# Multiplying zeros in eight waits of TensorE, in a four-round transformer kernel

## The reference, cut to what matters

```
x = x + layernorm(L0_attn(layernorm(x)))   # state-space mixer (conv, chunked scan, gate), then an FFN of 1024
x = x + layernorm(L0_ffn(layernorm(x)))    # x @ W.T plus a top-2-of-8 low-rank sum of rank 16
x = x + layernorm(L1_attn(layernorm(x)))   # causal attention, 16 heads of 16
x = x + layernorm(L1_ffn(layernorm(x)))    # top-4-of-64 experts of 64, capacity 32, plus two shared experts
```

## Time and profile before

| what | value |
|---|---|
| time, median of 3 runs | 1124.2 us (1123.39 to 1128.37) |
| profiled execution, first to last instruction | 1143.5 us |
| PE busy | 1018.9 us, 89% of the span |
| DVE, ACT, POOL busy | 782.8, 548.9, 394.8 us |
| mean granted TensorE clock | 0.958 |
| PE's share of the chain that ended last | 64% |

### The profile page before, as it was taken

How to read it: one execution, slowest core, us unless ns; L and a number is a source line. 1 busy time by engine, 2 the same in 40 slices (tenths; PEclk the granted TensorE clock), 3 DMA queues, 4 the chain that set the end, 5 groups by cost and what they waited for, 6 DMA issues and landing times.

```text
span 1143.5 us, 21218 instructions
## 1 busy us (share of the span) xinstructions
PE 1018.9 (89%) x7808; PEld 620.7 (54%) x7808; DVE 782.8 (68%) x1759; ACT 548.9 (48%) x1158; POOL 394.8 (35%) x605
## 2 busy tenths in 40 slices
PE   6999897899999998989998998999998998976466
PEld 3454554654555666654555666654555676655342
DVE  4888525678888646678887546779896546766135
ACT  3888411346887211456886212447986112421112
POOL 3566201132765101133674101234673001223442
PEclk9999898899999999999999999999998999988778
DMA  6889200003443000004443001004348304024727
GB/s 212 314 295 312 79 1 19 1 2 106 140 143 116 1 1 19 20 1 141 142 126 95 1 1 38 1 13 155 131 143 200 68 1 129 1 68 116 220 107 299
DMA packets 74743, 113.64 MB, mean 99 GB/s; under 512 B 6167, under 2 KB 64670, under 8 KB 73744
## 3 DMA queue, kind: packets, MB, share of 16 engines
q1 hardware_dynamic: 71952, 104.48, 29.3%
q0 software_dynamic: 1536, 3.60, 1.1%
q10 hardware_dynamic: 1152, 4.19, 0.9%
HBM read 93.46 MB, written 19.40 MB: 99 GB/s over the span
## 4 chain that ended last, share of the span: by engine, by line
PE 64%; DVE 14%; issue 8%; ACT 7%; POOL 3%; DMA 2%; another core or an unknown queue 2%; SPq 0%; DVEq 0%; POOLq 0%; ACTq 0%
PE bank L957 25%; PE bank L1033 4%; PE bank L1124 4%; PE bank L1280 3%; PE bank L1238 3%; PE bank L1141 3%; DVE hf L1830 2%; PE bank L970 2%; PE bank L1324 2%; PE bank L1327 2%; POOL rs L1656 2%; PE bank L1048 2%; PE bank L948 2%; PE bank L1379 1%
## 5 line engine op out<-in xcount | busy, mean ns | idle before, releaser
L957 PE MATMUL bank<-uT,w_in 128*128 128x512 f32 (+1 forms) x584 | 273.9, 608 | 6.2 <-DVE hf L1844 3.0
L1830 DVE SCALAR_TENSOR_TENSOR hf<-bank,conv_w,hf 128x510 f32<-128x510 f32 (+2 forms) x224 | 162.6, 744 | 34.6 <-ACT nmax L1504 20.0
L957 PEld LDWEIGHTS bank<-uT,w_in 128*128 128x128 f32 (+1 forms) x584 | 102.2, 188 | 126.1 <-issue 91.1
L1656 POOL TENSOR_TENSOR rs<-ve,half 128x2 f32<-128x2 f32 x56 | 39.0, 697 | 289.2 <-DVE ve L1974 289.1
L1487 ACT ACTIVATE hf<-bank,conv_b,conv_w 128x512 f32<-128x512 f32 x128 | 99.2, 775 | 53.1 <-PE bank L957 52.6
L1124 PE MATMUL bank<-hf 64*64 64x128 f32 (+3 forms) x2048 | 89.5, 308 | 14.4 <-issue 7.5
L1124 PEld LDWEIGHTS bank<-hf 64*64 64x64 f32 x2048 | 75.6, 135 | 44.4 <-issue 37.6
L957 PE MATMUL bank<-uT,w_gu 128*128 128x512 f32 x224 | 99.0, 593 | 0.0
L1465 ACT ACTIVATE xc<-bank 128x512 f32<-128x512 f32 x44 | 26.3, 597 | 119.3 <-PE bank L957 77.1
L2271 DVE TENSOR_REDUCE nmax<-bank 128x2 f32<-128x256 f32 (+1 forms) x128 | 65.4, 553 | 20.3 <-PE bank L1327 18.1
L957 PEld LDWEIGHTS bank<-uT,w_gu 128*128 128x128 f32 x224 | 42.3, 190 | 46.6 <-issue 45.9
(11 more groups left out here) (343 smaller groups left out, 2170.8 us busy)
## 6 DMA issues: line engine op xcount, KB each, us to landing
hf<-cum_dram SPq DMA_DIRECT2D x32, 384.0 KB, 3.5
dec<-cum_dram SPq DMA_DIRECT2D x32, 384.0 KB, 4.0
tmp<-cum_dram SPq DMA_DIRECT2D x32, 384.0 KB, 3.5
x<-cum_dram SPq DMA_DIRECT2D x32, 384.0 KB, 3.9
y_dram<-xf SPq DMA_DIRECT2D x16, 512.0 KB, 6.1
w_in<-in_w_in SPq DMA_DIRECT2D x1, 3584.0 KB, 11.7
w_in<-in_w_egu SPq DMA_DIRECT2D x6, 512.0 KB, 10.4
w_in<-y_dram ACTq DMA_DIRECT2D x5, 512.0 KB, 10.8
```

The costliest lines, as they stand in the source:

```text
L957: mm = pe.matmul(plan[key][0:n, :], w[:, k, cols], uT[:, k, :], start=k == 0, stop=k == DC - 1)
L1656: pool.tensor_tensor(rs[:, cols], ve[:, cols], half[:, cols], ALU.pow).then_inc(rstd_ready.sem, 1)
L1830: ins = dve.scalar_tensor_tensor(d, x, conv_w[:, j, TAPS - 1 - s:TAPS - s], d, ALU.mult, ALU.add)
```

## The change

A helper `multiply_zeros(key, n, r)` waits for its bank, issues `n` bf16 products of the zero tile with 512 zero columns, and raises the bank's counts itself, so that no other engine takes part. It is called at eight places of TensorE's program, with 79 products in all: 10 in the first round between `project_out` and the FFN's transposes; 12 in the first round's low-rank stage before the second half's transposes, and 5 and 16 after the last product of its first and of its second half; in the last round 8 at step 19 of the attention loop, 9 after the loop and before `add_o(7)`, 7 after the shared experts' first half, and 12 between `shared_down(0)` and `add_to_table`. Bank 6 or 7 holds the results, which nobody reads. Nothing is removed or moved.

```diff
+            if r == 0:
+                plan.use("zeros_ffn", 6, r)
             for j in range(2):
                 plan.use(("O", j), j, r)
...
+            if r == 0:
+                for n in range(3):
+                    plan.use(("zeros_lora", n), 7, r)
             plan.use(("T", "att", 0), 6, r)
...
             plan.use(("W", 0), 7, r)
+            if r == LAST:
+                for n in range(2):
+                    plan.use(("zeros_att", n), 6, r)
...
         plan.use(("W", 1), 6, LAST)
+        plan.use(("zeros_att", 2), 6, LAST)
         plan.use(("T", "moe", 1), 6, LAST)
...
         plan.use("pos", 6, LAST)
+        plan.use(("zeros_att", 3), 6, LAST)
         plan.use("table", 7, LAST)
...
+            def multiply_zeros(key, n, r):
+
+                pe.wait_ge(*plan.before(key, r))
+                for i in range(n):
+                    mm = pe.matmul(plan.of(key, r)[:, :], zeros_bf[:, :], zeros_wide, start=True, stop=True)
+                    if i == n - 2:
+                        mm.then_inc(plan.fills(key, r), 1)
+                mm.then_inc(plan.drains(key, r), 1)
...
                     for j in range(2):
                         route(j, r - 1)
+                else:
+                    multiply_zeros("zeros_ffn", 10, r)
                 for j in range(2):
                     transposes(pe, "ffn", 1, u, j, r)
...
+                    elif j == 1:
+                        multiply_zeros(("zeros_lora", 0), 12, r)
                     transposes(pe, "lora", 2, u, j, r)
...
+                    if r == 0:
+                        multiply_zeros(("zeros_lora", 1 + j), (5, 16)[j], r)
                     if r > 0 and j == 0:
                         shared_down(0, r - 1, (1,))
...
+                    if n == 19 and r == LAST:
+                        multiply_zeros(("zeros_att", 0), 8, r)
...
+                if r == LAST:
+                    multiply_zeros(("zeros_att", 1), 9, r)
                 add_o(7)
                 transposes(pe, "moe", 4, xf, 0, r)
...
             for g in range(2):
                 shared_hidden(g, 0, LAST)
+            multiply_zeros(("zeros_att", 2), 7, LAST)
             transposes(pe, "moe", 4, xf, 1, LAST)
...
             shared_down(0, LAST)
+            multiply_zeros(("zeros_att", 3), 12, LAST)
             add_to_table(LAST)
             shared_down(1, LAST)
```

## The result

The changed kernel takes 1117.8 us (median of 8 runs), the kernel before 1123.8 us beside it; the ratio is 0.9931, with a 95% interval of 0.9911 to 0.995. By the ratio that is 7.7 us faster, with 5.6 to 10.0 us by its interval; the two medians by themselves lie 6.0 us apart. The forecast was 10.5 us and 1113.7 us, with a range of 1110 to 1119.5: the direction and the range held, the size was 2.8 us too large. A second measurement of the same kernel, further down, gave 0.9935.

The account below looks back on a forecast made before the run. The prediction took TensorE as the bound, busy 89% of the span and slowed by clock falls after waits. Terms of 2.0 + 6.0 + 1.3 + 1.2 = 10.5 us took the 1124.2 us median to 1113.7 us, range 1110 to 1119.5.

Parts of the forecast that it names:

- Term 1: First round's scan end: the FFN's first products run at the full clock, 2.0 us gained, at least 0.9.
- The row that spoke against it: Second round's scan end: `route` filled the wait, yet the clock fell for 3.42 us and the products took 4.85 us.
- Terms 2 and 3: First round's low-rank stage: second-half product 2.7 us faster, queries and keys 2.8, transposes at most 0.5; together 6.0 us.
- Term 4: Last round's `project_o(1)`: its 8 products fall from 3.19 to 1.9 us, 1.3 us gained.
- Term 5: Last round's `shared_down(1)`: 6.09 us falls to 3.72; counted as 1.2 us, between 0 and 2.4.
- POOL's limit: Tail: after the last gather at 1067.35 us, POOL's 16 scatters cannot end before 1089.2 us.
- the pairs' line: Tail: ACT's copy of `shared_down(1)`, then its exponentials and first expert pair; if it ends last, 2.4 us count.
- its inference about the unknown waits: Tail of the profiled execution: 19.25 us of wait without known releaser, inferred to be absent from timed runs.
- Some falls stay: Rival: the clock still falls where transposes and short waits follow the zeros; 1117 to 1120 us, chance 0.22.
- The gain is hidden: Rival: later rounds or the tail absorb gains; 1116.2 us without the last round's; hidden within 0.5%, chance 0.08.
- The blocks delay TensorE: Rival: blocks begun at the lower clock outlast their waits by 5.8 us, 1130 us; chance 0.04, shared with zeros doing nothing.
- Zeros are no work for the clock: Rival: nothing is gained, 1124 to 1130 us; chance 0.04, shared with blocks that delay.

Follow-up runs that it names:

- narrow: The change with all 79 products cut to 8 columns in place of 512; ratio 0.9995 to the kernel before.
- last_only: The change with only the 36 products of the last round, none in the first; ratio 0.9981 to the kernel before.
- scan_zeros: The change plus zeros at scan ends: 8 before the last convolution (all rounds), 2 and 3 around the FFN transposes (rounds 2 to 4); 1113.76 us, ratio 0.9904.
- pairs_late: The change plus 16 products of zeros between `shared_down(1)` and the expert pairs; ratio 0.9927 to the kernel before.
- again: The changed kernel itself, unaltered, measured and traced a second time; 1117.67 us, ratio 0.9935 to the kernel before.
- double: The change with twice the products in each of the eight blocks, 158 in all; ratio 1.0041 to the kernel before.
- tail_zeros: The change plus 52 products of zeros in the tail's wait for the loads of `y_dram`; ratio 0.9922 to the kernel before.

## Why the prediction was right, and where it was off

**The mechanism** held: zeros in the waits keep the clock, and without their columns (`narrow`) nothing is left of the gain.

**Term 1, scan end, 2.0 us.** L980 takes 3.62 us, against 5.71. From the start of `project_out`'s last products (L1219 in the changed kernel) to the end of the start column it takes 10.37 us in the nine traces with this block at its length, 12.05 in three of the four without and 12.87 in before's: 1.7 to 2.5 us, 1.9 on average. (The start column differs by as much, 138.2 against 140.1 us on average, but also holds what comes before, such as a fall within the scan in `last_only`.) The row that spoke against it was the second round's, where `route` fills the wait and the clock fell. The Trainium skill, "TensorE: Matmul & The Clock Gate", section "Part 4: PE-mode transpose", says that a transpose does not count as busy in the way that a product does; by it this term was 0.9. The measurement decides against that here: behind ten zeros the clock outlasted eight transposes and a wait of 0.85 us, in all nine traces (L980 3.62 us). At the other scan ends a fall at the transposes did occur (370.60 and 872.36 us above), though not in the third round of the same execution, and with the zeros of `scan_zeros` it is gone; which of those zeros it takes, and whether the transposes or the waits beside them let the clock fall, no run here shows.

**Terms 2 and 3, low rank, 6.0 us.** 72.6 to 66.5 us, 6.2 in each of the traces. Its parts don't stand apart as the prediction had them: the 12 alone are worth 3.8 us, the 5 and the 16 alone 4.6, together 6.2, not 8.4.

**Term 4, `project_o(1)`, 1.3 us.** 1.2: L1404 takes 1.99 us against 3.19.

**Term 5, `shared_down(1)`, 1.2 us.** This is the step that failed, as a size. In the profiled execution L1067 does take 3.69 us in the place of 6.09, 2.4 us, and none of it counts: POOL's line ends last, with room to spare (`pairs_late`, and `again` with 6.70 us and a tail no longer). The prediction had both lines, knew POOL's limit, and took the middle between 0 and 2.4 because the timed median agreed with the pairs' line. The lower end, 0, was right. So was its doubt that the clock may still fall in the 2.46 us wait, and its inference about the unknown waits.

**What the sum left out.** 1.9 + 6.2 + 1.2 are 9.3 us, and 7.7 were measured. The interval of 5.6 to 10.0 us holds both, so it is not shown that anything is missing. Of the other columns, route is 0.1 us longer with the last round's blocks, which is the 0.15 us wait behind the 7. Rounds 2 to 4 had 733.7 to 736.8 us in the three traces without the first round's blocks and without scan zeros, 735.0 to 738.2 in the seven with the first round's blocks; the means differ by 1.3 us, and the traces by 3.3 falls against 4.6 on average. The tail is 0.6 us longer on average in the traces with the 12 full-width products just ahead of it than in those without, before's own left out. Together that is 2.0 us, about the 1.6 between the two, but in both the sets of traces overlap, so it is not shown that the change causes more falls or a longer tail. The falls at the scan ends of rounds 2 to 4 come in different numbers in each execution, and the prediction said that they make runs differ by several us; it didn't put them into the sum.

**The rivals.** *Some falls stay* didn't come true at the places of the change: the stretches named by it are at 1.00. *The gain is hidden* came true for one term. It priced the last round's whole gain as lost, 1116.2 us, and the outcome, 1124.2 less 7.7 or 1116.5 us on the same base, lies by it, though project_o's 1.2 us do arrive. *The blocks delay TensorE* would have needed the lower clock ahead of a block; in the changed kernel no block began at it. What late blocks cost, `double` shows. *Zeros are no work for the clock* fell with the first window. Two small sums of these parts don't come out: the last round's terms are 1.3 + 1.2 = 2.5 us, not 2.4, and the terms at their upper ends add up to 11.7 us, not 12.1. The forecast rests on neither.

## What to carry to other kernels

A short wait on TensorE (here 1.2 to 3.5 us) can cost twice: once itself, and once in the products behind it if the clock falls there; work that nobody reads, sized to end just before the wait does, saves the second part. Look for such falls in every repetition of a stage, not only in the one where the profiled execution shows them: here the scan ends of rounds 2 to 4 were worth about another 4 us. And before counting what a faster product gives, follow its line to where two lines meet, and count it only if its own arrives last.

## What the runs showed of the hardware

Half the clock over 17 us of the tail cost nothing (`tail_zeros`): the loads behind POOL's scatters set the pace of the sums. A kernel's time followed its mean granted clock from run to run: the change's eight runs go from 1113.76 us at 0.987 to 1121.89 us at 0.978. The number of falls differs between executions of one program: in rounds 2 to 4 the changed kernel had four in one trace and five in the other, at some 1.3 us each. And a single profiled execution can hold waits that none of 13 others has, here some 17 us in the tail of before.
